# Adjacency loads of a graph and mixture-of-experts kernel: from quarter-wise loads and gathers to transfers over 128 partitions

## The reference

```python
mask = (adj > 0).astype(x.dtype)
deg  = jnp.sum(mask, axis=1, keepdims=True)
agg  = mask @ layernorm(x) / jnp.maximum(deg, 1.0)
self_f = layernorm(x) @ W_self + b_self
nb_f   = agg @ W_nb + b_nb
x = x + relu(concat([self_f, nb_f]) @ W_comb + b_comb)
# then a mixture of 8 experts, two per node
xf = layernorm(x); logits = xf @ Wg + bg
topk_scores, topk_idx = top_k(logits, 2); w = softmax(topk_scores)
h = gelu(einsum('nd,edh->neh', xf, W1) + b1); y = einsum('neh,ehf->nef', h, W2) + b2
x = x + sum of w * y over the two chosen experts
```

## Time and profile before

| | us |
|---|---|
| median of 3 runs | 504.6 |
| profiled execution, its own time | 503.99 |
| span of its profile | 502.2 |
| set-up, until the first matmul with a mask | 0 to 73.2 |
| main stage, until the last one | 73.2 to 332.0 |
| rest | 332.0 to 502.2 |

### The profile page before, as it was taken

How to read it: one execution, slowest core, us unless ns; L and a number is a source line. 1 busy time by engine, 2 the same in 40 slices (tenths; PEclk the granted TensorE clock), 3 DMA queues, 4 the chain that set the end, 5 groups by cost and what they waited for, 6 DMA issues and landing times.

```text
span 502.2 us, 12812 instructions
## 1 busy us (share of the span) xinstructions
PE 435.5 (87%) x4214; PEld 383.2 (76%) x4214; DVE 374.2 (75%) x1056; ACT 261.2 (52%) x403; POOL 328.7 (65%) x348
## 2 busy tenths in 40 slices
PE   5789999799999979999969998954999999997720
PEld 5578888688888868888848887843799999986610
DVE  2899654467779879797758788766677777779972
ACT  2566773144533534445435454233588888886630
POOL 3398585264665878877738876367777868665560
PEclk9999999999999989999979999995899999999975
DMA  8998799889995999799999997296865565598675
GB/s 216 272 292 251 210 228 284 234 236 279 279 279 159 294 280 281 209 292 302 299 295 267 297 310 228 87 286 214 264 194 175 176 178 178 169 337 339 198 220 167
DMA packets 48688, 122.48 MB, mean 244 GB/s; under 512 B 10601, under 2 KB 19693, under 8 KB 47600
## 3 DMA queue, kind: packets, MB, share of 16 engines
q1 hardware_dynamic: 26736, 64.09, 45.0%
q0 software_dynamic: 16144, 50.49, 33.5%
q10 hardware_dynamic: 5744, 7.08, 5.1%
HBM read 96.52 MB, written 26.93 MB: 246 GB/s over the span
## 4 chain that ended last, share of the span: by engine, by line
DVE 32%; PE 31%; DMA 14%; issue 9%; POOL 8%; ACT 3%; SPq 1%; DVEq 1%; ACTq 0%; POOLq 0%
PE bank L1342 8%; PE bank L1362 8%; DMA wst<-in_L_ffn_W_dram 8%; PE bank L1245 7%; DVE maskT L845 5%; POOL rs L633 3%; PE bank L1329 3%; DVE x_sb L930 2%; DVE xh L928 2%; DMA x_sb<-in_x_dram 2%; DVE w L982 2%; DMA stage<-in_adj_dram 2%; DVE st L934 2%; PE bank L1236 2%; ACT xh L725 2%
## 5 line engine op out<-in xcount | busy, mean ns | idle before, releaser
L1236 PE MATMUL bank<-z_flat,maskT 128*128 128x257 f16 x1024 | 231.3, 277 | 7.7 <-issue 7.6
L1237 PE MATMUL bank<-z_lo,maskT 128*128 128x256 f16 x1024 | 231.2, 276 | 0.0
L1236 PEld LDWEIGHTS bank<-z_flat,maskT 128*128 128x128 fp8e4 x1024 | 101.5, 99 | 21.6 <-issue 8.2
L651 POOL DMA_INDIRECT pair_out<-rows,enum x78 | 87.6, 1123 | 39.5 <-issue 18.3
L1237 PEld LDWEIGHTS bank<-z_lo,maskT 128*128 128x128 fp8e4 x1024 | 101.4, 99 | 12.8
L676 ACT ACTIVATE mask<-stage,m 128x2048 fp8e4<-128x2048 int32 x32 | 64.1, 2002 | 53.4 <-DMA stage<-in_adj_dram,gidx 39.7
L584 POOL DMA_INDIRECT dispatched<-rows,slot x64 | 66.4, 1038 | 28.0 <-issue 18.5
L573 POOL DMA_INDIRECT stage<-in_adj_dram,gidx x64 | 67.5, 1054 | 24.9 <-issue 13.3
L725 ACT ACTIVATE xh<-x_sb,nb,rs 128x256 f32<-128x256 f32 x32 | 19.2, 600 | 102.6 <-POOL nb L635 80.4
L633 POOL TENSOR_TENSOR rs<-ve,mhalf 128x1 f32<-128x1 f32 x32 | 39.8, 1245 | 49.4 <-DVE ve L939 49.1
L1342 PE MATMUL bank<-stage,w 128*128 128x256 f16 x468 | 59.7, 279 | 5.6 <-DVE stage L1115 5.3
(11 more groups left out here) (179 smaller groups left out, 604.9 us busy)
## 6 DMA issues: line engine op xcount, KB each, us to landing
stage<-in_adj_dram SPq DMA_DIRECT2D x256, 128.0 KB
stage<-dispatched SPq DMA_DIRECT2D x39, 260.0 KB, 3.0
wst<-in_L_ffn_W_dram ACTq DMA_DIRECT2D x16, 256.0 KB, 10.2
z_lo<-pair_out SPq DMA_DIRECT2D x4, 1024.0 KB, 7.1
dispatched<-pad SPq DMA_DIRECT2D x15, 260.0 KB
out_dram<-x_sb SPq DMA_DIRECT2D x28, 128.0 KB, 4.8
maskT<-pair_out SPq DMA_DIRECT2D x3, 1024.0 KB, 9.6
x_sb<-in_x_dram ACTq DMA_DIRECT2D x6, 256.0 KB, 11.4
```

The costliest lines, as they stand in the source:

```text
L651: gp.indirect_dma_start(out=yp_dram[:, :], out_offset=bass.IndirectOffsetOnAxis(ap=enum[:, a, s:s + 1], axis=0), in_=ysb[:, a, s, :], in_o ...
L1236: mm(acc[u % 2][:, 0:D + 1], a, z_hi[:, i, :], start=(i == 0), stop=False)
L1237: last = mm(acc[u % 2][:, 0:D], a, z_lo[:, i, :], start=False, stop=(i == NT - 1))
```

## The change

SP loads both buffers of a tile. Each row quarter b is one transfer of 512 KB with all 128 partitions as its destination; its source is 4 column quarters by 32 rows by 1024 columns. The waits are `s_mD` ahead of the two transfers of the even buffer and `s_mA` ahead of the two of the odd buffer, now both on SP. `gather`, its index column, its iotas and its calls on POOL go. The count that DVE waits for goes from 8 transfers to 2 (16 per transfer).

```diff
             def load_adj(t):
-                s = 2 * (t % 2)
-                if t >= 2:
-                    sp.wait_ge(s_mD, t - 1)
-                for b in range(2):
-                    for g in (0, 2, 1, 3):
-                        sp.dma_start(stage[Q * g:Q * g + Q, s, b, :], adj_v[t // B, t % B, g, :, b, :]).then_inc(s_adj[s], 16)
+                for half, made in ((0, s_mD), (1, s_mA)):
+                    s = 2 * (t % 2) + half
+                    if t >= 2:
+                        sp.wait_ge(made, t - 1)
+                    for b in range(2):
+                        sp.dma_start(stage[:, s, b, :], adj_v[t // B, t % B, :, :, 2 * half + b, :]).then_inc(s_adj[s], 16)
...
-            def gather(t):
-                s = 2 * (t % 2) + 1
-                if t >= 2:
-                    pool.wait_ge(s_mA, t - 1)
-                for b in (2, 3):
-                    gp.indirect_dma_start(
-                        out=stage[:, s, b - 2, :], out_offset=None, in_=adj_q[:, :],
-                        in_offset=bass.IndirectOffsetOnAxis(ap=gidx[:, 0:1], axis=0),
-                        element_offset=(b * NQ + t // B * P + t % B) * N).then_inc(s_adj[s], 16)
...
-                if k == 1:
-                    gather(0)
...
-                if k in (2, 4, 5, 7):
-                    gather((2, 4, 5, 7).index(k) + 1)
-            gather(5)
...
-                m = made_in(s)
-                if m is not None and m + 2 < NT:
-                    gather(m + 2)
...
-                dve.wait_ge(s_adj[s], 128 * (div(t, u, known, 0, 2) + 1))
+                dve.wait_ge(s_adj[s], 32 * (div(t, u, known, 0, 2) + 1))
```

More of the change, by code:

```diff
@@ L67, in gnn_moe_kernel @@
     out_v = out.rearrange("(g k c e) d -> g k c (e d)", g=G, k=NG, c=Q, e=B)
-    adj_q = adj.rearrange("n (g j) -> (n g) j", g=G)
     adj_v = adj.rearrange("(b k r e) (g j) -> k e g r b j", b=G, k=NG, r=Q, e=B, g=G)
@@ L114, in gnn_moe_kernel @@
         bcol = sb("bcol", [P, 2, KT], F32)
-        gidx = sb("gidx", [P, 1], I32)
         mhalf = sb("mhalf", [P, B], F32)
@@ L271, in gnn_moe_kernel @@
             "weights_transposed", "wT_copied", "weights_folded", "fold_hi", "fold_scales"))
-        s_gi = sem("gather_indices")
         s_fmx, s_fmr, s_fch, s_wf, s_bb, s_cp, s_cb = (sem(n) for n in (
@@ L552, in _ @@
             gp.iota(pad32[:, TOK:TOK + 1], [[0, 1]], base=2 * N, channel_multiplier=1).then_inc(s_pad, 1)
[L554 to L559, removed]
             def rstd(k):
@@ L614, in _ @@
                         normalise(t)
-                if k in (2, 4, 5, 7):
-                    gather((2, 4, 5, 7).index(k) + 1)
-            gather(5)
             pool.dma_start(b1c[:, :, :], b1.rearrange("e (t p) -> p e t", p=P), allow_slow_non_contiguous=True).then_inc(s_b12, 16)
-            self_and_const(0)
-            gather(6)
-            self_and_const(1)
+            for k in range(2):
+                self_and_const(k)
             LAST_POWERS = NT + X1
```

## The result

The changed kernel takes 903.85 us (median of 4 runs, 902.12 to 905.73) against 505.25 us before (4 runs): 1.787 times the time, 95% interval 1.781 to 1.793. The forecast was 955 us, range 870 to 1300, slower with 0.90. The direction and the mechanism held. The 955 us were 51 us too high: one term was 80 us too large, two were 27 and 8 us too small, and they cancelled in part.

What follows compares the result with a forecast made beforehand. PE was taken to bound the main stage, DMA close behind. With adjacency on four engines: 21 (x, weights) + 723 (adjacency) + 25 (other bytes) + 3.8 + 7.1 + 3 + 170.2 + 1.8 = 955 us, range 870 to 1300.

Steps and rivals of the forecast that it cites:

- What bounds: Main stage, 74 to 325 us: PE sets the pace, busy 236.4 of 251 us, DMA close behind at share 0.92.
- Four engines: Adjacency transfers: source outer count 4 allows at most 4 of 16 engines, each carrying 16.8 MB; 643 us undisturbed.
- The rate of one engine: Adjacency transfers: an undisturbed DMA engine carries 26.1 GB/s.
- The 80 us on top of 643: Adjacency transfers: engines writing quadrants of one side meet in shared lanes, raising 643 us to 723.
- Other bytes, 25 us: After 21 us: weights, dispatches and small transfers on the same four engines, 0.64 MB each, add 25 us.
- From the last landing to the last neighbour matmul, 13.9 us: End of main stage: mask, transpose and hand-overs 3.8 us, PE's last tile 7.1 us, plus 3 us.
- The rest: After the main stage: routing, dispatch and experts take 170.2 us, as before.
- Edits costed at nothing: Main stage: two waits a tile on SP's queue cost 0; fewer SP transfers are worth nothing by themselves.
- the signs: Changed profile: DMA share 0.25 to 0.35, mask waits 13 to 16 us a tile, PE idle 15 of 23, tail 170.
- sixteen engines: Adjacency transfers cut along the 128 destination rows, so faster: 490 us against 504.6; chance 0.08.
- A time of over 1300 us: Adjacency transfers: the four engines stay in step for most of the time, over 1300 us; chance 0.10.
- Sixteen engines with nothing gained: Main stage: rows spread well, but bytes were never later than PE can hide; within 0.5% of 504.6 us; chance 0.02.

Runs made afterwards that it cites:

- the version without the shape: Changed kernel with each row quarter as four 128 KB, 32-row transfers on SP, gathers still gone: 512.88 us, 0.985 of before; repeated 493.77 us, 0.978.
- the kernel one dimension away: Changed kernel with its source walked rows first, outer count 32 instead of 4, masks scrambled: 504.64 us, 0.963 of before.

## Why the prediction was right

1. *What bounds.* Right: main stage by PE with DMA close behind. With a quarter of the engines it became DMA alone.
2. *Four engines.* Right: rate and queue share go with the count at 2, 4 and 8, and at 32 PE sets the pace again. That an outer count of 4 gives four engines was an estimate of mine: before, only counts of 32 with a share of 1.02 to 1.03 were to be seen. The count is what was varied; that it is a number of engines is read from the share, since no row names them.
3. *The rate of one engine.* 26.1 GB/s from rows 7 and 10; measured 26.2 (105 / 4).
4. *The 80 us on top of 643.* Wrong, and the largest miss. The 723 us are 1.125 x 643, and no run shows the 1.125, my own factor for what two engines of one side lose to each other. Measured nearly alone the four run at 26.2 GB/s each (105 / 4), factor 1.00, and with two engines at 25.5 (51 / 2). The 216 GB/s for quadrants of one side came with 16 engines at work, at a share of 1.03; two engines of 26 GB/s ask for 52 of them. The term belongs at 0.
5. *Other bytes, 25 us.* Too small. From 21 us to the last landing at 712.6 us there are 691.6 us; 16.78 MB at 26.2 GB/s are 640; 52 us are left. From 200 to 600 us the adjacency lost 105 - 98 = 7 GB/s, 2.8 MB, to others of 6.9 MB in all (q0, q10, program), of which a quarter, 1.7 MB, ran on these engines if they spread evenly over the 16: they cost about 1.6 times their bytes (2.8 / 1.7), an estimate. That makes 25 into 40 us; 12 us I can't place.
6. *From the last landing to the last neighbour matmul, 13.9 us.* Measured 734.1 - 712.6 = 21.5. I had one tile left for PE; there were two. PE had stood 13.5 us before its transposes of line 1252, since DVE's rows waited for ACT, and ACT stood in its mask wait. Behind ACT's one wait of 20.8 us PE fell a tile behind. No run shows the 3 us that the sum adds there for a slower clock. What the changed kernel shows is a clock of 0.50 from 712 to 720 us, 0.90 from 720 to 726 and 1.00 from 726 to 735, and matmuls 0.21 us apart instead of 0.11 from 718.5 to 721.2 us: some 1.3 us in all, an estimate from 13 of them.
7. *The rest.* 170.2 us forecast, 903.9 - 734.1 = 169.8 measured.
8. *Edits costed at nothing.* SP's two waits: no cost seen, since the version without the shape has them and is faster than before. Gathers gone: I gave it no worth, and together with the single queue it brings 2.2%.

The sum in the measured sizes is 21 + 640 + 52 + 21.5 + 169.8 = 904 us. It meets the 903.9 of the span because the 52 us are what was left over, so this is no further proof. That the forecast came within 51 us is partly luck: without the 80 us of item 4 the same sum gives 875 us, 29 too low, and the 80 us, which the runs put at 0, made up for the terms that were too small.

Of the signs, the share (0.29) and the tail (169.8 us) came as forecast. The masks waited longer, (532.0 + 116.5) / 32 = 20.3 us a tile against 13 to 16. The first product with a mask came at 122.3 us instead of 73.2, so that a step took (734.1 - 122.3) / 32 = 19.1 us and not 23. PE idled half of it, not two thirds.

The rivals: sixteen engines was wrong for this kernel, and came out for the kernel one dimension away: 0.963 of before against the 0.97 priced, and ACT's waits for data fell to 1.6 us. The run without the shape shows that some 1.5% of that gain comes without the shape, from the single queue or the missing gathers. A time of over 1300 us, to which I gave 0.10, was wrong by item 4. Sixteen engines with nothing gained was wrong for both.

## What to carry over

Before judging a transfer by its size or its partitions, write down both sides as the instruction carries them and look at the slowest count of each: the smaller one, here always the source's, set how much of the 16 engines was used, 2, 4 or 8 of them by the shares of 12.6, 24.5 and 47.6%, and the time followed. A small count at the destination, or one that is no power of two, was not tried. If a change makes that count small, estimate the transfer time as bytes / (count x 26 GB/s) (23 to 26 were measured) and compare this with the pace of the stage. A DMA share near a round fraction of 16 (0.12, 0.25, 0.48) with masks waiting for data and an issuing queue that "takes" microseconds is the sign of it.

## What the runs showed of the hardware

- One DMA engine carried 26.2 GB/s of 4 KB rows if the 105 GB/s are divided by four, and 26.1 with sixteen at once (418 GB/s, larger rows for the most part).
- Sixteen engines on one side of SBUF: 216 GB/s. Two engines on one side (source outer count 2): 51 GB/s, 25.5 each, against 26.2 each for the four of the changed kernel.
- SP's issue of a 512 KB transfer takes 0.53 to 0.60 us; when the queue is full the same instruction lasts 4.9 us in the median and up to 11.9.
- POOL's one-column power (line 633 before, 606 after) took 1245 ns in the mean before and 618 ns after the change, row of the changed kernel:

```profile
L606 POOL TENSOR_TENSOR rs<-ve,mhalf 128x1 f32<-128x1 f32 x32 | 19.8, 618 | 492.4 <-DVE ve L909 492.4
```

The gathers around it are not the cause: without them it took 1339 ns in the version without the shape, and with them 620 ns in the run with only the even half changed. It was short (556 to 620 ns) in the three slowest kernels and long (1218 to 1339 ns) in all others. What it waits for inside was not tried.
